# Joining the softmax states of several heads side by side, in one kernel of graph layers

## What is computed

```python
alpha = jnp.einsum('ehd,ehd->eh', q[dst], k_e) / jnp.sqrt(jnp.float32(D))
m = jax.ops.segment_max(alpha, dst, num_segments=N)
a = jnp.exp(alpha - m[dst])
z = jax.ops.segment_sum(a, dst, num_segments=N)
attn = a / z[dst]
out = jax.ops.segment_sum(attn[:, :, None] * v_e, dst, num_segments=N)
```

## Time and profile before

| | us |
|---|---|
| median of 3 runs | 8214.33 (8205.5 to 8215.38) |
| the profiled execution | 8208.71 |
| its span, first to last instruction | 8206.6 |
| `conv`, first loop | 1085 |
| `conv`, second loop | 1086 |
| `conv`, last loop | 1479 |
| `angle`, loop | 1626 |

### The profile page before, as it was taken

The page is one execution under the profiler, slowest core; times in us unless marked ns, Lnnn a source line. Parts: engine busy times, 40 slices in busy tenths (PEclk is TensorE's granted clock), DMA queues, the critical chain, the costliest instruction groups (busy, mean ns, idle before and its releaser), DMA issues. The chain is left out here.

```text
span 8206.6 us, 130447 instructions
## 1 busy us (share of the span) xinstructions
PE 4943.2 (60%) x25679; PEld 3551.4 (43%) x25679; DVE 6211.7 (76%) x29225; ACT 4759.9 (58%) x13649; POOL 5280.9 (64%) x5272
## 2 busy tenths in 40 slices
PE   4103333258898578888477777739950277666660
PEld 1002222246666366666355555525630155455550
DVE  9807777748888578888388888866768588777775
ACT  0007888737777467777266666644534366556552
POOL 7767777457777277776465555407753477777773
PEclk8555555579999799999698899969975698888885
DMA  3335666424454244444243344426646333333330
GB/s 101 100 101 113 129 129 131 109 85 154 155 160 152 80 131 155 160 153 148 66 138 129 128 129 133 131 79 192 206 167 221 126 117 109 100 100 105 104 95 27
DMA packets 480674, 1036.07 MB, mean 126 GB/s; under 512 B 226926, under 2 KB 232237, under 8 KB 479879
## 3 DMA queue, kind: packets, MB, share of 16 engines
q1 hardware_dynamic: 316102, 720.08, 27.5%
q0 software_dynamic: 163904, 309.78, 14.6%
HBM read 557.39 MB, written 472.92 MB: 126 GB/s over the span
## 5 line engine op out<-in xcount | busy, mean ns | idle before, releaser
L1513 POOL DMA_INDIRECT xs<-tab,rec x1176 | 1161.4, 988 | 762.6 <-DVE cA L1655 291.7
L1515 POOL DMA_INDIRECT xd<-tab,rec x1176 | 1156.6, 984 | 358.5 <-issue 356.1
L1598 ACT ACTIVATE z<-p_a 128x512 f32<-128x512 f32 x1176 | 697.3, 593 | 545.4 <-PE p_a L1453 532.7
L1592 ACT ACTIVATE st<-xs,cb 128x128 f32<-128x128 f32 x2352 | 804.7, 392 | 197.5 <-DVEq L1704 197.2
L1453 PE MATMUL p_a<-ident,st 128*128 128x128 f32 x2352 | 509.7, 300 | 461.9 <-DVE st L1666 458.3
L1666 DVE SCALAR_TENSOR_TENSOR st<-st,cg 128x128 f32<-128x128 f32 x2352 | 721.9, 348 | 77.5 <-DVE norm L691 49.0
L1544 PE MATMUL p_a<-w_own,xt 128*128 128x256 f32 x2352 | 755.5, 405 | 21.4 <-ACT xt L1583 21.1
L1547 PE MATMUL p_y<-w_qk,xt 128*128 128x258 f32 x2352 | 764.5, 409 | 0.6 <-ACT xt L1583 0.5
L1655 DVE CUSTOM_DVE_ANT_0 junk<-p_y,xs 128x129 f32<-128x129 f32 x2352 | 584.2, 285 | 113.9 <-PE p_y L1547 111.8
L1453 PEld LDWEIGHTS p_a<-ident,st 128*128 128x128 f32 x2352 | 288.4, 147 | 800.8 <-DVE st L1666 741.9
L1457 PE MATMUL p_m<-w_val,z 128*128 128x128 f32 x2352 | 599.5, 338 | 0.0
(11 more groups left out here) (692 smaller groups left out, 16748.1 us busy)
## 6 DMA issues: line engine op xcount, KB each, us to landing
states<-st SPq DMA_DIRECT2D x168, 910.0 KB
own<-tab SPq DMA_DIRECT2D x168, 448.0 KB
tab<-o SPq DMA_DIRECT2D x168, 448.0 KB
in<-tab SPq DMA_DIRECT2D x168, 448.0 KB
runs<-run SPq DMA_DIRECT2D x112, 448.0 KB, 2.9
res<-out SPq DMA_DIRECT2D x112, 448.0 KB
tab<-out SPq DMA_DIRECT2D x112, 448.0 KB
angles<-st SPq DMA_DIRECT2D x56, 532.0 KB, 2.9
```

Of the source, the lines that this page charges most:

```text
L1513: pool.indirect_dma_start(xs[:, i, j, 0:D], None, table, bass.IndirectOffsetOnAxis(ap=rec[:, i, SRC, j : j + 1], axis=0)).then_inc(got_in[ ...
L1515: pool.indirect_dma_start(xd[:, i, j, :], None, table, bass.IndirectOffsetOnAxis(ap=rec[:, i, PLACE, j : j + 1], axis=0)).then_inc(got_in[ ...
L1592: ins = act.activation(state_of(r, j)[:, h, :], xs[:, c.slot(UB), j, 0:D], ACT.Copy, scale=co.b[:, c.slot(2), h, j : j + 1])
L1598: act.activation(z[:, c.slot(RING), j, :], p_a[two(c, j)][:], ACT.Copy).then_inc(st_copied, 1)
```

## The change

`merge_softmax` takes the heads in groups of n = min(H, 4): two groups of four in `angle`, one of two in `conv`. Each VectorE and ScalarE instruction covers a whole group, with n x 128 columns where it had 128. The single instruction that subtracted the maximum and took the minimum with 0 (L1287) becomes two, since the maximum is now another for each head. Each engine goes through the groups three times (turn and exponential, weights, output) instead of once for each head, so that all transposes of m and z come first. ScalarE copies the turned weights, VectorE did. The head's own share is multiplied before the wait for the matmuls and added after it. The four kinds of PSUM tile are separate, one for each group; `out_of` is gone. In `angle` all scratch behind the loop now lies in the rings `xs` and `edge`. Where lines were removed (they are in the listing above) the diff has a line of "...".

```diff
--- before.py
+++ after.py
@@ -1241,70 +1241,79 @@
     ASK, EXP = 2, 3
 
 
...
+def merge_softmax(k, sb, sem, ps_m, ps_z, ps_w, ps_o, co, tail, head, head_m, head_z, out, W):
 
 
     nc, H = k.nc, co.H
...
+    n = min(H, 4)
+    groups = range(H // n)
+    e, w, wt = sb("me", [P, H, P]), sb("mw", [P, H, P]), sb("mwt", [P, H, P])
+    top, mine, sum_, inv, was = [sb(x, [P, H]) for x in ("mtop", "mmine", "msum", "minv", "mwas")]
+    rowed, exped, exp_in, turned, weighed, untangled, summed, done = [
+        sem(x) for x in ("rowed", "exped", "exp_in", "turned", "weighed", "untangled", "msummed", "mdone")]
+    part = lambda t, g: t[:, g * n : (g + 1) * n]
+    side = lambda t: t[:, 0 : n * P].rearrange("p (h c) -> p h c", h=n)
+    over = lambda t: t[:].unsqueeze(1).to_broadcast([P, n, P])
+    each = lambda s, g, x: part(s, g).unsqueeze(2).to_broadcast([P, n, x])
     with nc.Block() as b:
 
         @b.tensor
         def _(pe):
...
+            for g in groups:
+                for h in range(n):
+                    pe.transpose(ps_m[g][:, h * P : (h + 1) * P], wide(co.m[:, g * n + h, J : J + 1], P), k.ident[:])
+                    ins = pe.transpose(ps_z[g][:, h * P : (h + 1) * P], wide(co.z[:, g * n + h, J : J + 1], P), k.ident[:])
+                ins.then_inc(rowed, 1)
+            for g in groups:
+                pe.wait_ge(weighed, g + 1)
+                for h in range(n):
+                    ins = pe.transpose(ps_w[g][:, h * P : (h + 1) * P], w[:, g * n + h, :], k.ident[:])
+                ins.then_inc(turned, 1)
+            for g in groups:
+                pe.wait_ge(untangled, g + 1)
+                for h in range(g * n, (g + 1) * n):
+                    ins = pe.matmul(ps_o[g][:, (h - g * n) * W : (h - g * n + 1) * W], wt[:, h, :], tail[:, h, :], start=True, stop=True)
+                ins.then_inc(summed, 1)
 
         @b.scalar
         def _(act):
...
+            for g in groups:
+                act.wait_ge(exp_in, g + 1)
+                act.activation(part(mine, g), part(mine, g), ACT.Exp)
+                act.activation(part(e, g), part(e, g), ACT.Exp).then_inc(exped, 1)
+            for g in groups:
+                act.wait_ge(turned, g + 1)
+                act.activation(part(wt, g), side(ps_w[g]), ACT.Copy).then_inc(untangled, 1)
 
         @b.vector
         def _(dve):
             step = Chain(dve, done)
...
+            for g in groups:
+                dve.wait_ge(rowed, g + 1)
+                step(dve.tensor_tensor(part(e, g), side(ps_m[g]), over(k.no_join), ALU.add))
+                step(dve.tensor_reduce(part(top, g), part(e, g), AX.X, ALU.max))
+                step(dve.tensor_tensor(part(top, g), part(top, g), part(head_m, g), ALU.max))
+                step(dve.tensor_tensor(part(e, g), side(ps_m[g]), each(top, g, P), ALU.subtract))
+                step(dve.tensor_scalar(part(e, g), part(e, g), 0.0, None, ALU.min))
+                step(dve.tensor_tensor(part(mine, g), part(head_m, g), part(top, g), ALU.subtract))
                 dve.nop().then_inc(exp_in, 1)
...
+            for g in groups:
+                dve.wait_ge(exped, g + 1)
+                step(dve.tensor_tensor(part(w, g), part(e, g), over(k.join), ALU.mult))
+                step(dve.tensor_tensor(part(w, g), part(w, g), side(ps_z[g]), ALU.mult))
+                step(dve.tensor_reduce(part(sum_, g), part(w, g), AX.X, ALU.add))
+                step(dve.tensor_tensor(part(was, g), part(mine, g), part(head_z, g), ALU.mult))
+                step(dve.tensor_tensor(part(sum_, g), part(sum_, g), part(was, g), ALU.add))
+                step(dve.tensor_scalar(part(sum_, g), part(sum_, g), 1.0e-30, None, ALU.max))
+                step(dve.reciprocal(part(inv, g), part(sum_, g)))
+                step(dve.tensor_tensor(part(was, g), part(was, g), part(inv, g), ALU.mult))
+                step(dve.tensor_tensor(part(w, g), part(w, g), each(inv, g, P), ALU.mult))
                 dve.nop().then_inc(weighed, 1)
...
+            for g in groups:
+                o = part(out, g)
+                step(dve.tensor_tensor(o, part(head, g), each(was, g, W), ALU.mult))
+                dve.wait_ge(summed, g + 1)
+                step(dve.tensor_tensor(o, o, ps_o[g][:, 0 : n * W].rearrange("p (h w) -> p h w", h=n), ALU.add))
 
 
 
@@ -1794,7 +1803,7 @@
                 pool.indirect_dma_start(also[:], None, k.res, row, bounds_check=k.NR - 1, oob_is_err=False).then_inc(fetched, 16)
                 pool.wait_ge(fetched, 48)
 
...
+        merge_softmax(k, sb, sem, [p_t[0]], [p_t[1]], [p_y[0]], [p_y[1]], co, state_of(RING - 1, J - 1), halves(kept_row[:, 0 : 2 * D]),
                       kept_row[:, 2 * D : 2 * D + H], kept_row[:, 2 * D + H : KEPT], fix, D)
         f_turned, f_copied, f_made, f_out, f_low, f_exp, f_put, f_done = [
             sem(n) for n in ("f_turned", "f_copied", "f_made", "f_out", "f_low", "f_exp", "f_put", "f_done")]
@@ -2486,6 +2495,14 @@
                 walk(k, dve, one, SCORE, 5)
 
 
+        room, used = [t[:].rearrange("p r j d -> p (r j d)") for t in (xs, edge)], [0, 0]
+
+        def sb(n, s):
+            size, at = s[-1] * (s[1] if len(s) == 3 else 1), int(n in ("me", "mw"))
+            used[at] += size
+            t = room[at][:, used[at] - size : used[at]]
+            return t.rearrange("p (a b) -> p a b", a=s[1]) if len(s) == 3 else t
+
         kept_row, mine, fix = sb("kept_row", [P, KEPT_A]), sb("mine", [P, D]), sb("fix", [P, H, V])
         mt, zf, mf, of, gf = sb("mt", [P, D]), sb("zf", [P, D + 1]), sb("mf", [P, D]), sb("of", [P, D]), sb("gf", [P, 2])
         cleared, fetched = sem("cleared"), sem("fetched")
@@ -2501,7 +2518,7 @@
                 pool.indirect_dma_start(mine[:], None, table, row, bounds_check=k.NR - 1, oob_is_err=False).then_inc(fetched, 16)
                 pool.wait_ge(fetched, 32)
 
...
+        merge_softmax(k, sb, sem, p_t, p_q[0:2], p_q[2:4], p_o, co, heads(value_of(UB - 1, J - 1), V), heads(kept_row[:, 0 : H * V], V),
                       kept_row[:, H * V : H * V + H], kept_row[:, H * V + H : KEPT_A], fix, V)
         f_turned, f_copied, f_made, f_out, f_low, f_exp, f_put, f_done = [
             sem(n) for n in ("f_turned", "f_copied", "f_made", "f_out", "f_low", "f_exp", "f_put", "f_done")]
```

More of the change, by code:

```diff
@@ L1241 @@
     ASK, EXP = 2, 3
-def merge_softmax(k, sb, sem, ps, co, tail, head, head_m, head_z, out, W):
+def merge_softmax(k, sb, sem, ps_m, ps_z, ps_w, ps_o, co, tail, head, head_m, head_z, out, W):
     nc, H = k.nc, co.H
[L1248 to L1256, removed]
+    n = min(H, 4)
[8 more added lines that the diff above has]
+    each = lambda s, g, x: part(s, g).unsqueeze(2).to_broadcast([P, n, x])
     with nc.Block() as b:
@@ L1280, in _ @@
             step = Chain(dve, done)
[L1281 to L1288, removed]
-                dve.nop().then_inc(exp_in, 1)
[L1290 to L1300, removed]
-                dve.nop().then_inc(weighed, 1)
[L1302 to L1307, removed]
@@ L1795, in _ @@
                 pool.wait_ge(fetched, 48)
-        merge_softmax(k, sb, sem, [p_t[0], p_t[1], p_y[0]], co, state_of(RING - 1, J - 1), halves(kept_row[:, 0 : 2 * D]),
+        merge_softmax(k, sb, sem, [p_t[0]], [p_t[1]], [p_y[0]], [p_y[1]], co, state_of(RING - 1, J - 1), halves(kept_row[:, 0 : 2 * D]),
                       kept_row[:, 2 * D : 2 * D + H], kept_row[:, 2 * D + H : KEPT], fix, D)
@@ L2502, in _ @@
                 pool.wait_ge(fetched, 32)
-        merge_softmax(k, sb, sem, [p_t[0], p_t[1], p_q[0]], co, heads(value_of(UB - 1, J - 1), V), heads(kept_row[:, 0 : H * V], V),
+        merge_softmax(k, sb, sem, p_t, p_q[0:2], p_q[2:4], p_o, co, heads(value_of(UB - 1, J - 1), V), heads(kept_row[:, 0 : H * V], V),
                       kept_row[:, H * V : H * V + H], kept_row[:, H * V + H : KEPT_A], fix, V)
```

## The result

| | before, us | after, us |
|---|---|---|
| median | 8214.9 (4 runs, 8205.5 to 8216.9) | 8164.5 (4 runs, 8159.8 to 8166.2) |
| ratio | | 0.994, 95% interval 0.9923 to 0.9957 |
| `angle` join, first transpose to last add | 54.93 | 20.94 |
| each `conv` join | 14.23 | 9.62 |

The kernel is 50.4 us faster by the medians; 48.3 were forecast. The interval of the ratio is wide: it allows 35 to 63 us, so the whole times can't tell the forecast from a gain some 13 us off it. The lengths of the joins can: they are 34.0 + 3 x 4.6 = 47.8 us shorter.

The account below looks back on a forecast made before the run. The joins were taken as serial chains between barriers, 97.6 us of the span. Gains of 34.4 us in `angle` and 13.9 in `conv` summed to 48.3, from 8214.3 to 8166.0 us, range 8152 to 8178.

Parts of the forecast that it names:

- The bound: Joins stand between barriers, all on the path: 97.6 us together, 1.2% of the span, the most the change can give.
- The two halves: Gains forecast for the `angle` join, 34.4 us, and for the three `conv` joins together, 13.9 us.
- The price list: Prices for the joins' steps: VectorE 0.72 us over 512 columns, min 0.46, small step 0.195, TensorE pass 0.215.
- the tail: End of the `angle` join after VectorE's last scale: TensorE's transposes and matmuls and a last add, some 4.9 us.
- the sum: Terms of the `angle` join after the change, from first transposes to last add: 20.5 us.
- the sign that it is never idle for over 0.1 us: In `angle`, VectorE was never to idle over 0.1 us between the first turned tables and the last weights.
- rival A: Wide operands in the joins are dear, an element costing twice: gain 41 us, 8173 us, chance 0.08.
- rival B: Denser TensorE work lifts the clock inside the join: 6 us at most, 3 if only `angle`, 8163 us, chance 0.07.
- My test for B: A granted clock above 0.5 inside the join would speak for the clock rising there.
- rivals C and D: C: last `conv` stage loses its clock, 8257 us, chance 0.02; D: 32 to 65 us lost in loops, 8214, chance 0.02.
- The drawn interval: Range for the whole time, 8152 to 8178 us, from the earlier runs' spread, A's and B's prices and 4 for drift.

Follow-up runs that it names:

- half-changed kernels: Against the kernel before, the grouped join in `conv` alone (8194.4 us, ratio 0.9978) or in `angle` alone (8176.0 us, ratio 0.9955).
- the fillers: Changed kernel plus 64 and 20 extra transposes, or 32 and 10 matmuls, while TensorE would wait in `angle`: join 19.00 and 19.01 us.
- one group after the other: Changed kernel, but the second group of four begins only when the first is out: `angle` join 27.8 us.
- the repeat: The changed kernel run again without an edit: median 8160.8 us of five, ratio 0.9935 to the kernel before, `angle` join 20.94 us.
- the shorter join: Changed kernel without the min and mask product, with 44 and 12 extra transposes in `angle`: `angle` join 17.17 us, each `conv` join 8.83.

## Why the prediction was right

*The bound.* The joins stood alone between barriers, and what they lost came out of the total: 47.8 us in the profile of the changed kernel, 50.4 us between the medians. The two halves separate as forecast (34.4 and 13.9 predicted; 34.0 and 13.8 by the joins; 36.2 and 17.8 by the medians of the half-changed kernels, both within their intervals). The forecast set the gain at 45 to 50 us: the joins' 47.8 lie in that band, the 50.4 between the medians just above it. That the medians came within 1.5 us of the forecast is partly luck, since their interval is 14 us wide either way; the joins within 0.5 us are not.

*The price list.* A 512-column step was put at 0.72 with its wait and took 0.72 (0.69 and the gap); the `min` 0.46, took 0.46; ScalarE's copy 0.59, took 0.60; the tail 4.85 us, took 4.80. The whole `angle` join was 0.4 us longer than the sum. Most of that is a term that the sum lacked: three times VectorE goes from one half of a group to the next, and each time it stands still for 0.15 us, where the sum had the 0.04 of an ordinary step. So the sign that it is never idle for over 0.1 us was not met. The rest is that small steps take 0.20 and not 0.195, L1308 0.21. The `conv` join came out at 9.62 against 9.59.

*Repeated operands (rival A)* cost nothing: L1296, L1302 and L1310 read an operand repeated over heads or columns and take 0.69 us like L1303 and L1304, which read plain operands of the same width. The row L2462, from which I took no surcharge, was the right neighbour. This is shown by the rows after the change.

*The clock (rival B)* was half right, and here my reasoning had a gap. I took the 0.50 of the old join as a sign that the clock would stay down. It rose at the end of the sixteen dense transposes, too late for them and too early for the matmuls:

```profile
8132.00:8133.00 1.00, 1.00 (x6) 0.69 (x4) 0.93 (x3) 0.00 (x0) 0.00 (x0) 0.50 0.00 0
8133.00:8134.00 1.00, 0.10 (x1) 0.00 (x0) 0.93 (x3) 0.00 (x0) 0.00 (x0) 0.91 0.00 0
...
8136.00:8137.00 1.00, 0.00 (x0) 0.00 (x0) 0.92 (x3) 0.00 (x0) 0.00 (x0) 0.80 0.00 0
8137.00:8138.00 1.00, 0.00 (x0) 0.00 (x0) 0.82 (x3) 0.35 (x2) 0.00 (x0) 0.50 0.00 0
```

So it was worth nothing, as the forecast had it, but for another reason. The kernel with the grouped join in `angle` alone shows the same from the other side: there the clock stayed at 0.50 throughout, and the join took the same 20.94 us. My test for B, a granted clock above 0.5 inside the join, would have called it true; the right test is the clock under the passes that lie on the path. With the fillers the clock was up under the tail and gave 1.94 us; I had put 3 us on `angle`, as I counted the first eight transposes in, which the clock can't reach.

*The loops (rivals C and D).* The last `conv` loop took 1477 us at 0.88, so C did not happen. The `angle` loop was 1644 to 1653 us in five profiles (the changed kernel twice, the two halves, one group after the other), against 1638 in the one profile of before. In the medians there is no trace of a loss: the joins' 47.8 us are all there, and 2 to 4 us more. I take it for the loops' own variation. For that speaks the stretch ahead of the first join, where nothing changed: it lasts 2783.1 us in the profile of before and 2784.6 to 2792.5 in the five others, so the one profile of before is the shortest there too. But it isn't shown for the `angle` loop: all five kernels keep the scratch in the rings, and no run has the old scratch with the new join. A second profile of before on a fast chip, or such a run, would show it.

*The drawn interval.* 8152 to 8178 held the median and all four runs; of the five runs of the repeat one took 8178.6. Of its 26 us, 10 are the run-to-run spread, 13 the prices of A and B, neither of which was due, and the rest drift.

## What to carry to other kernels

A chain of small dependent steps between barriers can be priced from its own rows to a few per cent: start cost and element cost from two widths of one form, plus the handovers, each priced from its own row. When such a chain is repeated for each head, widening its steps saves most (27 us here, at 512 columns), overlapping the groups the rest (7 us), and after that the order in which a queue takes the groups decides how long the tail is (0.7 us). Which engine makes a copy is worth little while both fit beside another engine's work.

## What the runs showed of the hardware

- Transposes alone can raise TensorE's clock. After or near the end of sixteen in 3.6 us the granted clock went from 0.50 to 1.00 in the first profile of the change, in the repeat, in the kernel with group one's matmuls first and in the one with groups of two; it stayed at 0.50 in `angle` alone and with VectorE's copies, with the same sixteen. What decides between the two isn't shown. In the repeat it came 0.3 us before their end, and the last two transposes took 0.29 and 0.27 us instead of 0.42. With 64 transposes or 32 matmuls as fillers it was up in both, and both joins took 19.0 us.
- Once up it stays for a while after the work ends (3.5 us in the first profile, with TensorE idle), and in the shorter join it fell while TensorE was busy without a gap, 1.7 us after the end of an idle 1.3 us. The Trainium skill ("TensorE: Matmul & The Clock Gate", Part 4) says that transposes don't count as busy for the clock; these runs differ, and the measurement decides.
- Two chips ran the same kernel in 8212 and in 10,168 us (medians), with the same durations inside the joins. A comparison of loops across these chips would have been worthless, one of joins was exact to 0.1 us.
